# Attention sums of a graph network: indirect stores of a pair tied to TensorE's matmul groups, and TensorE's signals reduced from 16 to nine per pair

## Chip, cores and metric

One core of a Trainium2 chip runs the whole program in one launch. The metric is the device time in microseconds of one execution. Engines are called PE (TensorE), DVE (VectorE), ACT (ScalarE), POOL (GpSimd) and SP (SyncE), as in the profile; L1208 is line 1208 of the kernel.

## What is computed

Two graph layers over 100,000 nodes with 64 features and 25,000 edges sorted by target node, each followed by a residual and a layer norm. The change lies in the first layer, an attention layer with four heads and a self loop at each node:

```python
alpha = a_src_n[src2] + a_dst_n[dst2] + a_edge
alpha = jnp.where(alpha >= 0, alpha, NEG_SLOPE * alpha)
ae = jnp.exp(alpha - segment_max(alpha, dst2)[dst2])
attn = ae / segment_sum(ae, dst2)[dst2]
agg = segment_sum(xw[src2] * attn[:, :, None], dst2)
proj = (agg.reshape(n, H * C) + bias) @ Wp + bp
h = x + elu(proj)
out = layernorm(h) * gamma + beta          # then x = layernorm(x + out)
```

## The kernel before

The program has stages with a barrier between them. The **dense stage** computes the first layer for all nodes as if they had only their self loop, and gathers the rows of both ends of all edges with indirect loads that POOL issues (L277). The weights of all edges follow. Then comes the stage of the **attention sums** (names that begin with first_), which this case is about: for the nodes that have edges it forms the sums over them and writes the finished rows over the dense ones in the node table x1 in HBM (x_table in the rows). Last comes the stage of the second layer (second_), which gathers from that table.

The attention sums treat 50 units of 512 edges as 25 **pairs**. A pair stands in tiles of 128 partitions by 512 columns: 64 features of a unit from the lower half of the edges, and 64 of one from the upper half. `slots(PAIRS, 5, slot)` writes every engine's program out as 30 **slots**. In slot u each engine does its part of several pairs at different depths: `u.back(2)` is the pair two slots before. The order within a slot is the order of the calls in each engine's `slot` function, and engines meet only through semaphores.

- DVE in slot u: `own_part` (L1379) and four `product`s (L1385), one per head, write five operands `first_zb` of pair u; two `scan`s (L1392) run the weighted sums along the edges of pair u-1; `refine_roots`, `scale`, `flag`, `add_scaled` and `finish` (L1445) make the output rows of pair u-3 and u-4; `elu` and `residual` (L1411) go on with pair u-1. `finish` fills one of four row buffers `first_xr` and signals `xr_made`.
- PE in slot u: `spread` (L1231) broadcasts a head's weights over 128 partitions for a `product` of DVE, four times; `head_sum` (L1245) multiplies the five operands into one PSUM bank; `difference` (L1237) serves pair u+1; `centre` (L1251), `variance` (L1256, eight passes of two columns) and `to_rows` (L1264 and L1265) serve pair u-2.
- ACT copies, squares and takes exponentials: `square` (L1329) waits for `centre` of the same pair, `guess_roots` (L1343) for `variance`.
- POOL writes the rows of pair u-4 in slot u: eight indirect stores (here **scatters**, L1208) of 128 rows of 65 values each, addressed by `first_rows`. It waits once, for `xr_made` of the pair, and issues the eight one after the other.
- SP loads the masks and weights (`first_mask`, `first_wt`) of pair u+1 when the scans of pair u-1 are done.

PE signals by incrementing a semaphore at the end of a matmul: four times for `spread`, once for `difference`, five times for `head_sum`, once each for `centre` and `variance`, four times for `to_rows`, 16 in all for a pair.

POOL has the same kind of work in the dense stage. There a function `after_matmuls` already ties the gathers to PE's groups, here in its own words:

```python
for j in range(8):
    after_matmuls(2 * e - 3 + j // 4, j % 4)
    gather_pair(pool, e, j)
```

Of the kernel before, what the change touches and what calls it, by code (L numbers as in the profile page):

```python
# [35 lines left out]
PAIRS = UNITS // 2  # L36
# [135 lines left out]
def gnn(nc, x, gidx, drow, dblk, eaT, ea3, p64, p128, out):  # L172
# [14 lines left out]
    with ExitStack() as ctx:  # L187
# [939 lines left out]
        with ExitStack() as ph:  # L1127
# [72 lines left out]
            @block.gpsimd  # L1200
            def _(pool):
                last_row = pool.alloc_register("last_row")
                pool.reg_mov(last_row, N - 1)

                def scatter(u, s):
                    b, at = u.off % 4, (PAIRS - 1 - u.off) * 8 + 4 * s
                    for j in range(4):
                        pool.indirect_dma_start(  # L1208
                            out=x1, out_offset=bass.IndirectOffsetOnAxis(ap=first_rows[:, at + j:at + j + 1], axis=0),
                            in_=xr[b][:, 2 * j + s, :], in_offset=None, bounds_check=last_row, oob_is_err=False)\  # L1210
                            .then_inc(scattered[b], 16)

                def slot(u):
                    u = u.back(4)
                    if u.valid(PAIRS):
                        pool.wait_ge(xr_made, u.count(1))
                        scatter(u, 0)
                        scatter(u, 1)

                slots(PAIRS, 5, slot)  # L1220
                for b in range(4):
                    pool.wait_ge(scattered[b], 128 * ((PAIRS + 3 - b) // 4))

            @block.tensor
            def _(pe):
# [14 lines left out]
                def head_sum(u, n):  # L1240
                    b = u.off % 2
                    if n == 0:
                        atleast(pe, scanned, 2 * u.count(-1))
                    pe.wait_ge(z_made, u.count(0) * (H + 1) + (n + 1))
                    nc.tensor.matmul(pY[b][:, :], Mhead[:, n - 1, :] if n else Mblk[:, :], zb[n][:, :],  # L1245
                                     start=(n == 0), stop=(n == H)).then_inc(z_used, 1)

# [12 lines left out]
                def to_rows(u, j):  # L1260
# [3 lines left out]
                    nc.tensor.matmul(pG[:, c], hc[:, c], CG[:, :], start=True, stop=True)  # L1264
                    nc.tensor.matmul(pC[:, c], xd[u.off % 4][:, c], Cm, start=True, stop=True).then_inc(rows_made, 1)  # L1265

# [38 lines left out]
            def _(act):  # L1305
# [3 lines left out]
                def copy_targets(u):  # L1309
                    atleast(act, rows_made, u.count(-3) * 4)  # L1310
                    nc.scalar.activation(xd[u.off % 4][0:64, :], XT[64:128, columns(u, 0)], ACT.Identity,
# [14 lines left out]
                def square(u):  # L1326
                    act.wait_ge(hc_made, u.count(1))
                    atleast(act, rows_made, u.count(0) * 4)
                    nc.scalar.activation(sq[:, :], pH[:, :], ACT.Square, bias=ncbeta[:, :])  # L1329
# [44 lines left out]
            def _(dve):  # L1374
                def own_part(u):
                    dve.wait_ge(w_loaded[u.off % 2], u.halves(1) * 64)
                    dve.wait_ge(xd_copied, u.count(1))
                    atleast(dve, z_used, u.count(-1) * (H + 1) + 1)
                    nc.vector.scalar_tensor_tensor(zb[0][:, :], mask[u.off % 2][:, :], 1.0, xd[u.off % 4][:, :],  # L1379
                                                   ALU.subtract, ALU.mult).then_inc(z_made, 1)  # L1380

                def product(u, h):
                    dve.wait_ge(spread_made, u.count(0) * H + (h + 1))
                    atleast(dve, z_used, u.count(-1) * (H + 1) + (h + 2))
                    nc.vector.tensor_tensor(zb[1 + h][:, :], pB[h % 2][:, :], df[u.off % 2][:, :], ALU.mult).then_inc(z_made, 1)  # L1385

                def scan(u, s):
                    b, half = u.off % 2, slice(64 * s, 64 * s + 64)
                    dve.wait_ge(z_used, u.count(1) * (H + 1))
                    atleast(dve, e_made, u.count(-1))  # L1390
# [36 lines left out]
                def scale(u):  # L1427
                    dve.wait_ge(roots_made, u.count(1))
                    dve.wait_ge(rows_made, u.count(1) * 4)
                    atleast(dve, yc_made, u.count(0))  # L1430
# [709 lines left out]
```

## Time and profile before

| | us |
|---|---|
| median of 3 runs | 1848.58 |
| lowest, highest | 1843.01, 1853.82 |
| the profiled execution | 1859.29 |
| its span | 1857.5 |
| PE busy | 1280.9 (69%) |
| DVE busy | 1202.5 (65%) |
| ACT busy | 876.8 (47%) |
| POOL busy | 994.5 (54%) |
| L1208, 200 scatters, busy | 202.3 |
| granted clock of TensorE, mean share of full | 0.805 |

The attention sums lie between about 800 and 1215 us of the span. An instruction's row names the line, the operation, the tile that it writes and those that it reads. The bracket at the end is how long its engine was idle before it and what ended that. "remote" there means that the profile names no instruction of this core whose end fits the moment at which the wait ended. Starts and durations of matmuls are modelled.

### The profile page before, as it was taken

To read this page: it belongs to the slowest core of one execution; us is meant where nothing else is said; L and a number is where in the kernel's file an instruction comes from. 1 tells how busy PE (TensorE), PEld (TensorE's weight loads), DVE (VectorE), ACT (ScalarE), POOL (GpSimd) and SP (SyncE) were. 2 spreads that over 40 slices of the span, in tenths; PEclk is the share of its full clock that TensorE was granted. 3 is DMA by queue.
4 is the path that set the end of the run, shared out by engine and by line. 5 is a ranking of instruction groups with operands and counts; after the bars stand their busy time and mean duration, and the time that the engine had idled before them with its cause. 6 is when DMAs were issued, how large, how long until landed. Compare 5 with 4: busy or idle time off the path is not lost. (4 is left out here: it accounts for less than half of the span.)

```text
span 1857.5 us, 19719 instructions
## 1 busy us (share of the span) xinstructions
PE 1280.9 (69%) x5229; PEld 791.0 (43%) x5253; DVE 1202.5 (65%) x2284; ACT 876.8 (47%) x1944; POOL 994.5 (54%) x993
## 2 busy tenths in 40 slices
PE   5887787787787782068888887427667666666662
PEld 4555555555555551023444444314343344333331
DVE  4767667667667676857776777318475566665574
ACT  2667667657666673034444443405343344443341
POOL 5655555555555530003555555555676666776665
PEclk9898898888899896579888888558777777777776
DMA  4445545555545542011111111113122222222310
GB/s 114 138 149 170 156 142 169 160 152 163 165 142 162 163 135 95 0 28 30 44 51 46 44 43 44 27 38 69 36 67 50 59 61 62 61 61 50 74 46 22
DMA packets 162058, 161.98 MB, mean 87 GB/s; under 512 B 82994, under 2 KB 99681, under 8 KB 161948
## 3 DMA queue, kind: packets, MB, share of 16 engines
q1 hardware_dynamic: 130300, 130.80, 22.8%
q0 software_dynamic: 31648, 29.92, 7.7%
q8 instruction: 43, 0.70, 0.2%
q14 instruction: 67, 0.55, 0.1%
HBM read 66.88 MB, written 83.27 MB: 81 GB/s over the span
## 5 line engine op out<-in xcount | busy, mean ns | idle before, releaser
L277 POOL DMA_INDIRECT ids_pairs<-in_x_dram,gix x392 | 383.7, 979 | 296.9 <-PE bank L605 149.5
L1208 POOL DMA_INDIRECT x_table<-first_xr,first_rows x200 | 202.3, 1011 | 331.8 <-DVE first_xr L1445 273.3
L1605 POOL DMA_INDIRECT second_raw<-x_table,gix x196 | 201.0, 1026 | 142.7 <-PE twin L1711 60.8
L1611 POOL DMA_INDIRECT out_dram<-second_orow,last_rows x196 | 202.5, 1033 | 70.8 <-issue 58.5
L587 PE MATMUL twin<-AC,dense_hb 128*128 128x256 f32 x784 | 198.1, 397 | 37.7 <-DVE dense_hb L741 25.5
L579 PE MATMUL bank<-dense_xT,Mblk 128*128 128x512 f32 x196 | 125.6, 727 | 71.5 <-ACT dense_rl L670 53.2
L587 PEld LDWEIGHTS twin<-AC,dense_hb 128*128 128x128 f32 x784 | 147.0, 198 | 64.9 <-DVE dense_hb L741 31.4
L749 DVE TENSOR_REDUCE dense_v<-dense_q 128x8 f32<-128x512 f32 x98 | 66.7, 681 | 110.7 <-ACT dense_q L645 108.9
L1245 PE MATMUL twin<-first_zb,Mhead 128*128 128x512 f32 x200 | 129.3, 736 | 0.0
L595 PE MATMUL bank<-prm,dense_xT 128*128 128x128 f32 x784 | 118.5, 300 | 2.4 <-DVE dense_yc L784 2.3
L1385 DVE TENSOR_TENSOR first_zb<-twin,first_df 128x512 f32<-128x512 f32 x100 | 66.6, 686 | 79.0 <-remote 58.8
L595 PEld LDWEIGHTS bank<-prm,dense_xT 128*128 128x128 f32 x784 | 110.9, 218 | 4.7 <-DVE dense_yc L784 3.5
L681 ACT ACTIVATE dense_hq<-twin 128x512 f32<-128x512 f32 x98 | 58.7, 599 | 98.2 <-PE twin L587 63.6
L1787 ACT ACTIVATE second_decay<-twin 128x512 f32<-128x512 f32 x25 | 14.9, 597 | 184.7 <-issue 158.6
L729 DVE TENSOR_REDUCE dense_v<-dense_hq 128x8 f32<-128x512 f32 x98 | 66.8, 682 | 29.9 <-issue 15.7
L695 ACT ACTIVATE dense_lrow<-bank 12x512 f32<-12x512 f32 x50 | 29.3, 587 | 120.1 <-remote 115.1
L570 PEld LDWEIGHTS bank<-prm,ids_rows 128*128 128x128 f32 x392 | 58.1, 162 | 64.2 <-issue 64.2
L784 DVE TENSOR_TENSOR dense_yc<-dense_yb,bank 128x512 f32<-128x512 f32 x98 | 66.6, 679 | 26.2 <-issue 26.2
L741 DVE SCALAR_TENSOR_TENSOR dense_hb<-dense_xT,nbeta,dense_gb 128x512 f32<-128x512 f32 x98 | 73.7, 752 | 11.8 <-issue 0.5
L675 ACT ACTIVATE dense_xT<-bank,prm 128x512 f32<-128x512 f32 x98 | 67.3, 687 | 28.7 <-remote 28.7
L579 PEld LDWEIGHTS bank<-dense_xT,Mblk 128*128 128x128 f32 x196 | 35.3, 215 | 99.9 <-issue 78.1
L1108 DVE TENSOR_REDUCE d_s<-XT 128x8 f32<-128x512 f32 x50 | 31.9, 678 | 70.3 <-ACT XT L1077 57.5
(360 smaller groups left out, 3072.5 us busy)
## 6 DMA issues: line engine op xcount, KB each, us to landing
x_table<-dense_yc SPq DMA_DIRECT2D x98, 260.0 KB
ids_rows<-in_x_dram SPq DMA_DIRECT2D x98, 256.0 KB
out_dram<-dense_orow SPq DMA_DIRECT2D x98, 256.0 KB
XT<-dense_turned SPq DMA_DIRECT2D x50, 256.0 KB
target_rows<-first_xr SPq DMA_DIRECT2D x50, 128.0 KB
ids_pairs<-in_x_dram,gix POOLq DMA_INDIRECT x392
second_targets<-target_rows SPq DMA_DIRECT2D x49, 128.0 KB
first_mask<-mask_rows SPq DMA_DIRECT2D x50, 64.0 KB
```

The source lines that it names most:

```text
L277: pool.indirect_dma_start(out=pairs[e % 2][:, j % 4, F * (j // 4):F * (j // 4) + F], out_offset=None, in_=x, in_offset=bass.IndirectOffset ...
L579: nc.tensor.matmul(pP[:, :], Mblk[:, :], xT[u.off % 4][:, :], start=True, stop=True).then_inc(p_made, 1)
L587: last = nc.tensor.matmul(pGC[b][:, j * 256:(j + 1) * 256], hb[b][:, j * 128:(j + 1) * 128], AC[:, :], start=True, stop=True)
L595: last = nc.tensor.matmul(pX[:, c], xT[u.off % 4][:, c], Cm, start=True, stop=True)
L675: nc.scalar.activation(xT[u.off % 4][:, :], pT[:, :], ACT.Identity, bias=c128("beta")).then_inc(x_copied, 1)
L729: nc.vector.tensor_reduce(v[b][:, 0:8], hq[b][:, :, :], AX.X, ALU.add).then_inc(v1_made, 1)
L741: nc.vector.scalar_tensor_tensor(hb[b][:, :], xT[u.off % 4][:, :], nbeta[:, :], gb[:, :], ALU.add, ALU.add)\
L749: nc.vector.tensor_reduce(v[b][:, 8:16], q2[b][:, :, :], AX.X, ALU.add).then_inc(s2_made, 1)
L1208: pool.indirect_dma_start(out=x1, out_offset=bass.IndirectOffsetOnAxis(ap=first_rows[:, at + j:at + j + 1], axis=0), in_=xr[b][:, 2 * j + ...
L1245: nc.tensor.matmul(pY[b][:, :], Mhead[:, n - 1, :] if n else Mblk[:, :], zb[n][:, :], start=(n == 0), stop=(n == H)).then_inc(z_used, 1)
L1605: pool.indirect_dma_start(out=raw[u.off % 3][:, 2 * j + s, :], out_offset=None, in_=x1, in_offset=bass.IndirectOffsetOnAxis(ap=gix[:, at:a ...
L1611: pool.indirect_dma_start(out=out, out_offset=bass.IndirectOffsetOnAxis(ap=last_rows[:, at:at + 1], axis=0), in_=orow[u.off % 4][:, 2 * j ...
```

## The change

POOL's scatter function calls a new `after_matmuls` before each of the eight scatters. The scatters of pair k are issued while the engines work on pairs k+4 and k+5, and six of the calls wait, counted for pair k+5: scatter 2 (counting from 0) for `z_used`, that is for all head sums up to pair k+4; scatters 3, 4, 6 and 7 for the first, second, third and fourth `spread` of pair k+5; scatter 5 is tied to `hc_made`, the `centre` of pair k+3. Scatters 0 and 1 have no wait of their own. For the last five pairs there is no pair k+5 and nothing is tied.

`head_sum` signals only with its last matmul, and `to_rows` only with its last: nine signals for a pair in place of 16. All counts that wait on them are rewritten. Where DVE waited, before overwriting an operand `first_zb`, for the head sum of the pair before that read this operand, it now waits in `own_part` for all head sums of that pair, and the products no longer wait for `z_used`.

```diff
--- before.py
+++ after.py
@@ -1202,9 +1202,19 @@
                 last_row = pool.alloc_register("last_row")
                 pool.reg_mov(last_row, N - 1)
 
+                def after_matmuls(u, part):
+                    if u.valid(PAIRS):
+                        if part == 2:
+                            pool.wait_ge(z_used, u.count(0))
+                        if part in (3, 4, 6, 7):
+                            pool.wait_ge(spread_made, H * u.count(0) + {3: 1, 4: 2, 6: 3, 7: 4}[part])
+                        if part == 5:
+                            pool.wait_ge(hc_made, u.count(-1))
+
                 def scatter(u, s):
                     b, at = u.off % 4, (PAIRS - 1 - u.off) * 8 + 4 * s
                     for j in range(4):
+                        after_matmuls(u.back(-5), 4 * s + j)
                         pool.indirect_dma_start(
                             out=x1, out_offset=bass.IndirectOffsetOnAxis(ap=first_rows[:, at + j:at + j + 1], axis=0),
                             in_=xr[b][:, 2 * j + s, :], in_offset=None, bounds_check=last_row, oob_is_err=False)\
@@ -1242,8 +1252,10 @@
                     if n == 0:
                         atleast(pe, scanned, 2 * u.count(-1))
                     pe.wait_ge(z_made, u.count(0) * (H + 1) + (n + 1))
-                    nc.tensor.matmul(pY[b][:, :], Mhead[:, n - 1, :] if n else Mblk[:, :], zb[n][:, :],
-                                     start=(n == 0), stop=(n == H)).then_inc(z_used, 1)
+                    last = nc.tensor.matmul(pY[b][:, :], Mhead[:, n - 1, :] if n else Mblk[:, :], zb[n][:, :],
+                                            start=(n == 0), stop=(n == H))
+                    if n == H:
+                        last.then_inc(z_used, 1)
 
                 def centre(u):
                     pe.wait_ge(h_made, u.count(1))
@@ -1262,7 +1274,9 @@
                         atleast(pe, yc_made, u.count(0))
                     c = slice(j * 128, (j + 1) * 128)
                     nc.tensor.matmul(pG[:, c], hc[:, c], CG[:, :], start=True, stop=True)
-                    nc.tensor.matmul(pC[:, c], xd[u.off % 4][:, c], Cm, start=True, stop=True).then_inc(rows_made, 1)
+                    last = nc.tensor.matmul(pC[:, c], xd[u.off % 4][:, c], Cm, start=True, stop=True)
+                    if j == 3:
+                        last.then_inc(rows_made, 1)
 
                 def slot(u):
                     if u.static() and u.count(0) == 0:
@@ -1307,7 +1321,7 @@
                     name=nc.get_next_instruction_name(), engine=mybir.EngineType.Activation, act_func_set_id=EXP_AND_LN))
 
                 def copy_targets(u):
-                    atleast(act, rows_made, u.count(-3) * 4)
+                    atleast(act, rows_made, u.count(-3))
                     nc.scalar.activation(xd[u.off % 4][0:64, :], XT[64:128, columns(u, 0)], ACT.Identity,
                                          bias=c128("beta")[64:128, :])
                     nc.scalar.activation(xd[u.off % 4][64:128, :], XT[64:128, columns(u, 1)], ACT.Identity,
@@ -1325,7 +1339,7 @@
 
                 def square(u):
                     act.wait_ge(hc_made, u.count(1))
-                    atleast(act, rows_made, u.count(0) * 4)
+                    atleast(act, rows_made, u.count(0))
                     nc.scalar.activation(sq[:, :], pH[:, :], ACT.Square, bias=ncbeta[:, :])
                     nc.scalar.activation(hc[:, :], pH[:, :], ACT.Identity, bias=ncbeta[:, :]).then_inc(sq_made, 1)
 
@@ -1375,18 +1389,17 @@
                 def own_part(u):
                     dve.wait_ge(w_loaded[u.off % 2], u.halves(1) * 64)
                     dve.wait_ge(xd_copied, u.count(1))
-                    atleast(dve, z_used, u.count(-1) * (H + 1) + 1)
+                    atleast(dve, z_used, u.count(0))
                     nc.vector.scalar_tensor_tensor(zb[0][:, :], mask[u.off % 2][:, :], 1.0, xd[u.off % 4][:, :],
                                                    ALU.subtract, ALU.mult).then_inc(z_made, 1)
 
                 def product(u, h):
                     dve.wait_ge(spread_made, u.count(0) * H + (h + 1))
-                    atleast(dve, z_used, u.count(-1) * (H + 1) + (h + 2))
                     nc.vector.tensor_tensor(zb[1 + h][:, :], pB[h % 2][:, :], df[u.off % 2][:, :], ALU.mult).then_inc(z_made, 1)
 
                 def scan(u, s):
                     b, half = u.off % 2, slice(64 * s, 64 * s + 64)
-                    dve.wait_ge(z_used, u.count(1) * (H + 1))
+                    dve.wait_ge(z_used, u.count(1))
                     atleast(dve, e_made, u.count(-1))
                     atleast(dve, crossed, u.count(0) * 2 + (1 - s))
                     nc.vector.tensor_tensor_scan(ys[b][half, ::-1], mask[b][half, ::-1], pY[b][half, ::-1],
@@ -1426,7 +1439,7 @@
 
                 def scale(u):
                     dve.wait_ge(roots_made, u.count(1))
-                    dve.wait_ge(rows_made, u.count(1) * 4)
+                    dve.wait_ge(rows_made, u.count(1))
                     atleast(dve, yc_made, u.count(0))
                     nc.vector.tensor_tensor(yb[:, :, :], pG[:, :].rearrange("p (r f) -> p r f", f=F),
                                             w[:, 0:8].unsqueeze(2).to_broadcast([128, 8, F]), ALU.mult).then_inc(scaled, 1)
```

POOL's program around the stage, before: the last pair of the attention sums and what comes behind (first_xr_made is the signal of `finish`).

```order
L1208 DMA x_table<-first_xr,first_rows 100000x65 [waits first_xr_made]
L1208 DMA x_table<-first_xr,first_rows 100000x65 x7
L1127 UNCONDITIONAL_BRANCH [waits first_scattered2,first_scattered3,first_scattered1,first_scattered0]
L1598 UNCONDITIONAL_BRANCH [waits barrier_Pool_Activation_PE_DVE_SP_gather]
L1638 DMA second_lead<-x_table,gix 128x65 [waits second_cleared]
```

POOL after the change, from the stage's first row on: the first pair.

```order
L1200 UNCONDITIONAL_BRANCH [waits barrier_Pool_Activation_PE_DVE_SP_gather]
L1218 DMA x_table<-first_xr,first_rows 100000x65 [waits first_xr_made]
L1218 DMA x_table<-first_xr,first_rows 100000x65
L1218 DMA x_table<-first_xr,first_rows 100000x65 [waits first_z_used]
L1218 DMA x_table<-first_xr,first_rows 100000x65 [waits first_spread_made] x2
L1218 DMA x_table<-first_xr,first_rows 100000x65 [waits first_hc_made]
L1218 DMA x_table<-first_xr,first_rows 100000x65 [waits first_spread_made] x2
```

The eight scatters keep their order and number; six of the seven that followed freely are now tied to one signal of PE each.

DVE, before, from a place in the middle of the stage: the beginning of a slot (twin is the PSUM tile that `spread` or `head_sum` wrote).

```order
L1411 TENSOR_TENSOR first_hb<-first_gb,first_xd 128x512 [waits first_xd_copied,first_g_made,first_hc_made]
L1379 SCALAR_TENSOR_TENSOR first_zb<-first_mask,first_xd 128x512 [waits first_z_used,first_xd_copied,first_w_loaded1]
L1385 TENSOR_TENSOR first_zb<-twin,first_df 128x512 [waits first_z_used,first_spread_made] x2
L1392 SCALAR_TENSOR_TENSOR first_ys<-first_mask,first_start,twin 64x512 [waits first_crossed,first_e_made,first_z_used]
L1399 COPY first_start<-first_ys 64x1 [waits first_scanned]
L1420 TENSOR_TENSOR first_off<-first_ve,first_halved 128x16 [waits first_root_steps]
```

DVE at the same place after the change.

```order
L1424 TENSOR_TENSOR first_hb<-first_gb,first_xd 128x512 [waits first_xd_copied,first_g_made,first_hc_made]
L1393 SCALAR_TENSOR_TENSOR first_zb<-first_mask,first_xd 128x512 [waits first_z_used,first_xd_copied,first_w_loaded1]
L1398 TENSOR_TENSOR first_zb<-twin,first_df 128x512 [waits first_spread_made] x2
L1405 SCALAR_TENSOR_TENSOR first_ys<-first_mask,first_start,twin 64x512 [waits first_crossed,first_e_made,first_z_used]
L1412 COPY first_start<-first_ys 64x1 [waits first_scanned]
L1433 TENSOR_TENSOR first_off<-first_ve,first_halved 128x16 [waits first_root_steps]
```

No instruction of DVE moved; the products lost their wait for first_z_used.

## Rows read from the trace of the kernel before

**Rows 1.** Busy time by stretch (us, busy and count by engine, PEclk, DMA share, GB/s).
```profile
853.00:1149.00 296.00, 247.62 (x878) 124.54 (x877) 204.62 (x360) 124.51 (x257) 162.69 (x160) 0.84 0.17 44
1017.00:1028.00 11.00, 10.72 (x47) 5.42 (x46) 10.17 (x19) 6.33 (x14) 8.07 (x8) 1.00 0.22 57
1028.00:1048.00 20.00, 12.44 (x42) 5.83 (x41) 9.88 (x18) 5.96 (x13) 8.07 (x8) 0.75 0.13 35
1048.00:1061.00 13.00, 13.00 (x47) 7.02 (x48) 10.18 (x19) 6.27 (x14) 8.21 (x8) 0.85 0.22 52
1150.00:1215.00 65.00, 28.46 (x124) 22.48 (x124) 24.01 (x52) 27.41 (x58) 39.44 (x40) 0.58 0.13 31
```

**Rows 2.** Who waited for whom, 850 to 1150 us: total us, times, longest.
```profile
ACT first_sq L1329 <- remote: 61.8, 7, 9.8
DVE first_zb L1385 <- remote: 58.8, 7, 9.3
```

**Rows 3.** GpSimd in order of time, 1016 to 1050 us (start, us, instruction, idle).
```profile
1017.72 0.97 POOL L1208 DMA_INDIRECT x_table<-first_xr,first_rows  x1 [3.17 <-DVE first_xr L1445]
...
1026.95 0.97 POOL L1208 DMA_INDIRECT x_table<-first_xr,first_rows  x1 [0.30 <-issue]
1028.75 0.97 POOL L1208 DMA_INDIRECT x_table<-first_xr,first_rows  x1 [0.83 <-DVE first_xr L1445]
1030.03 1.27 POOL L1208 DMA_INDIRECT x_table<-first_xr,first_rows  x1 [0.30 <-issue]
1031.60 0.97 POOL L1208 DMA_INDIRECT x_table<-first_xr,first_rows  x1 [0.30 <-issue]
...
1037.99 0.97 POOL L1208 DMA_INDIRECT x_table<-first_xr,first_rows  x1 [0.30 <-issue]
1049.16 0.97 POOL L1208 DMA_INDIRECT x_table<-first_xr,first_rows  x1 [10.20 <-DVE first_xr L1445]
```

**Rows 4.** VectorE in order of time, 1016 to 1043 us.
```profile
1016.76 0.68 DVE L1445 TENSOR_TENSOR first_xr<-first_yc,first_wf 128x512 f32<-128x512 f32 x1
...
1019.93 0.69 DVE L1379 SCALAR_TENSOR_TENSOR first_zb<-first_mask,first_xd 128x512 f32<-128x512 bf16 x1 [0.51 <-DMA first_mask<-mask_rows]
1020.54 1.28 DVE L1385 TENSOR_TENSOR first_zb<-twin,first_df 128x512 f32<-128x512 f32 x2
...
1027.80 0.68 DVE L1445 TENSOR_TENSOR first_xr<-first_yc,first_wf 128x512 f32<-128x512 f32 x1
...
1030.99 0.69 DVE L1379 SCALAR_TENSOR_TENSOR first_zb<-first_mask,first_xd 128x512 f32<-128x512 bf16 x1 [0.53 <-DMA first_mask<-mask_rows]
1040.95 1.29 DVE L1385 TENSOR_TENSOR first_zb<-twin,first_df 128x512 f32<-128x512 f32 x2 [9.27 <-remote]
```

**Rows 5.** TensorE matmuls in order of time, 1016 to 1043 us.
```profile
1019.95 0.60 PE L1231 MATMUL twin<-first_wt,headsel 24*128 24x512 bf16 x2 [0.28 <-DMA first_mask<-mask_rows]
...
1026.06 0.95 PE L1256 MATMUL bank<-prm,first_sq 128*128 128x2 f32 x8
...
1028.70 1.02 PE L1245 MATMUL twin<-first_zb,Mhead 128*128 128x512 f32 x2
...
1031.01 0.60 PE L1231 MATMUL twin<-first_wt,headsel 24*128 24x512 bf16 x2 [0.40 <-DMA first_mask<-mask_rows]
```

**Rows 6.** ScalarE in order of time, 1016 to 1043 us.
```profile
1030.00 0.27 ACT L1343 ACTIVATE first_ve<-bank,eps 128x8 f32<-128x8 f32 x1 [1.65 <-remote]
...
1041.03 0.69 ACT L1329 ACTIVATE first_sq<-bank,ncbeta 128x512 f32<-128x512 f32 x1 [9.83 <-remote]
```

**Rows 7.** Dense stage, order of time, 350 to 362 us: TensorE.
```profile
354.59 1.03 PE L614 MATMUL bank<-dense_eab,WalE 16*12 16x512 f32 x4
```

**Rows 8.** Dense stage, same stretch: GpSimd.
```profile
358.18 0.94 POOL L277 DMA_INDIRECT ids_pairs<-in_x_dram,gix  x1 [0.30 <-issue]
```

**Rows 9.** Dense stage, same stretch: ScalarE.
```profile
360.21 1.19 ACT L695 ACTIVATE dense_lrow<-bank 12x512 f32<-12x512 f32 x2 [5.83 <-remote]
```

**Rows 10.** ScalarE in the last slots, 1160 to 1190 us.
```profile
1181.48 0.27 ACT L1343 ACTIVATE first_ve<-bank,eps 128x8 f32<-128x8 f32 x1 [10.58 <-remote]
```

## The prediction

> **What bounds the kernel now.** I read first how long a slot of the attention sums takes, then what the engines wait for in it, and last the order of time around one wait.
>
> In steady state the stage gives one pair per slot. From 853 to 1149 us POOL issues 160 scatters, that is 20 pairs, in 296 us [rows 1]: 14.8 us per slot. But slots differ. One from 1017 to 1028 takes 11.0 us, with PE busy 10.72 us at full granted clock and DVE busy 10.17: both full. The next takes 20 us and holds no more work (DVE 9.88 us busy), the one after 13 us, at a granted clock of 0.85 [rows 1]. So 11.0 us is what the work needs, and 296 - 20 x 11.1 = 74 us is lost in 20 slots (11.1 rather than 11.0, as a slot's loads and waits vary a little).
>
> The waits say where: seven waits of DVE's first product of a slot for "remote", 58.8 us in all, and seven of ACT's square, 61.8 us, which run beside them [rows 2]. Seven of some 9 us, and behind each a slot at reduced clock, which costs the rest: 58.8 + 7 x 2 = 73 us.
>
> The order of time shows what "remote" is. At 1031.0 PE does the two spreads that the products wait for; they end at 1031.6 [rows 5]. DVE's own part began at 1030.99, so the products could begin at 1031.6; they begin at 1040.95 [rows 4]. ACT's square, which waits for a later matmul, begins within 0.1 us of them [rows 6]. The variance matmuls ended at 1027.0 [rows 5] and ACT's reader of them began at 1030.00 [rows 6], while it was idle. So the work was done and its **signals were held**, several together, to be let go together. Meanwhile POOL issued scatters: 1028.75 to 1038.96, each 0.97 to 1.27 us long and 0.3 us apart; the held products begin 2.0 us after the last of them has ended [rows 3, 4]. In the slot before, POOL's eight scatters began at 1017.72 and the spreads of 1019.95 reached DVE without loss: its products begin at 1020.54, right behind its own part [rows 3 to 5]. So scatters alone do not hold a signal. What differs: in the second case a scatter (1026.95 to 1027.92) ran while the variance matmuls ended, and POOL paused only 0.83 us before the next eight [rows 3, 5]. Then PE added signals, 16 in a slot, faster than they came through (that of the variance at 1030.0, those of the spreads at 1040.9), so the row grew until POOL stopped. I take the held row of signals as the bound of this stage, and the overlap of POOL's trains with PE's signals as its cause.
>
> **The change part by part.**
>
> Nine signals for 16: no matmul, load or operand moves. PE is not shown waiting on its own signals in the 11 us slot, so by the rows the direct worth is nothing. The Trainium skill ("TensorE: Matmul & The Clock Gate", The cost: per-tile semaphore tail) says that increments serialize at about 26 ns each; 7 x 25 pairs would give an estimate of 4.6 us, and the sum would be that much lower. No row here shows it. What the smaller number does by the rows is to keep the held row short: between the variance and the first spread of the next slot there stood the head sums' last two and four of to_rows; now one of each.
>
> The six waits of POOL: 120 in all, for 20 pairs. In an undisturbed slot they cost nothing. Scatter 0 leaves 0.24 us after `finish` has ended, at +0; scatter 2 followed at about +2.85 (1031.60 against 1028.75) [rows 3]; the last head sum ends 1.0 us after scatter 0 begins (1028.70 + 1.02 against 1028.75) and the next spreads at +2.9 [rows 3, 5], so the signals for scatters 2, 3 and 4 are there or all but there when POOL comes to them, and those for the later ones likewise, since POOL needs 1.28 us per scatter. The cover is POOL's own pace; were it gone, each wait would delay one scatter, and behind it only `finish` waits, for a buffer four pairs old.
>
> In a slot whose signals are held, the waits are what counts. Scatters 0 and 1 still go at once (1028.75 to 1031.30). Scatter 2 now needs the last head sum's signal, which stands in the held row, so POOL stops at 1031.30 where it went on to 1038.96. How long after a stop is the row let go? The near rows give 2.0 us here, and 1.1 us in the dense stage: the last gather ended at 359.12, and ACT's L695, which had waited 5.83 us for matmuls that ended at 355.6, began at 360.21 [rows 7 to 9]. So the signals arrive at 1032.4 to 1033.3. New here is that DVE's own part waits for the same head sum; it can only begin then, and the products 0.6 us later, 1033.0 to 1033.9 against an undisturbed 1031.6: 1.4 to 2.3 us. If the head sum's signal slips through alone and starts scatter 2 with the spreads still held, one scatter (1.27) is added: up to 3.6 us. Below, the bound is 0, that the row is never held. I take 1.9 us, near the middle of the first pair, since its upper end is measured in this stage. DVE has 0.5 us of slack in a slot (its wait for `first_mask`, 0.53 [rows 4]), which I leave out, as the loads shift too. Such a wait is a fifth of the present one, and PE idles for 2 us instead of 7, so I also drop the slot at reduced clock.
>
> How many slots are so disturbed? Now it is seven of 20, each followed by a long gap of POOL (10.20 us [rows 3]) that clears the way for two. After the change the gap is short, so the pattern returns sooner: between every slot and every other. I take two in three. Mean slot: 11.1 + 2/3 x 1.9 = 12.4 us; 20 slots 247 us; **gain 296 - 247 = 49 us**.
>
> The end, 1150 to 1215 us [rows 1]: the last five pairs are not tied, and the 10.58 us wait of ACT there stays [rows 10]. With one signal of to_rows for four, the row is shorter behind it: gain 0 to 3 us, I take 1. The dense and the second-layer stages are untouched: 0.
>
> Sum: 49 + 1 = 50 us. The profiled execution took 1859.3 us (span 1857.5), 10.7 above the median, and would take 1809; from the median, 1848.6 - 50 = **1799 us**.
>
> **The rivals.** A difference of 0.5%, 9 us, is about what a measurement of this kernel can tell from none.
>
> B. *Signals are no longer held at all.* The overlap of train and variance signal may need the long unbroken row of scatters, and the shorter row of signals may never build up. For it: six of POOL's eight scatters now come behind a signal that has come through. Against: scatters 6 and 7 still fall where they fell, beside the variance matmuls. Every slot 11.1: gain 74, 1775 us or, with the end, 1774.
>
> C. *Held more often and longer.* Every slot is disturbed, and the row is let go as late as 2.8 us: 13.9 us per slot, 278 us, gain 18, 1831 us. For it: the dense stage, where POOL's gathers are tied in the same manner, still shows a wait of 5.83 us [rows 9]. Against: there the gathers before 359.12 went on in spite of the held row; here scatter 2 waits for a member of it.
>
> D. *Nothing that can be told.* If what holds the signals is not POOL's train but, say, the traffic of the stores already issued, the same seven waits stay: 1848.6, give or take 9.
>
> E. *Slower: tied scatters hold the next signal.* Each tied scatter begins at the moment a PE signal arrives, the next signal comes during it, and is held until POOL has stopped: a chain of six, each 1.27 us of scatter and 1.1 to 2.0 us of release. With 2.55 us for the first two, a slot would be 2.55 + 6 x 2.8 = 19.4 us, loss 20 x 4.6 = 92 us, 1940 us. It decides from the point where a step takes more than (14.8 - 2.55)/6 = 2.0 us. For it: a train takes 10.2 of 11 us, so POOL has 0.83 us to spare [rows 3], and any wait that is late by more pushes the next train. The Trainium skill ("DMA: Bandwidth & Descriptors", Rules for kernel authors) has a rule on this side: issue a transfer early and wait for it late. Against it: the slot from 1017 us, in which the spreads ended within a train and nothing was held [rows 3 to 5].
>
> **How the numbers follow.** A, my forecast, 0.50; its own range, mean slots of 11.7 to 13.2 us, is 1786 to 1816. B 0.22, C 0.14, D 0.08, E 0.06. The predicted time is A's. The range takes in A, B (its end is 1774, so 1773) and C with some more: to 1838; outside lie D, E and little else, less than 0.2. Faster by over 0.5%: A, B and most of C, 0.85. Within 0.5%: D and the rest of C, 0.09. Slower: 0.06.
>
> **What the profile of the changed kernel would show.** The seven "remote" waits of 9 us before L1398 (now the products) gone, and in their place waits of 1 to 3 us before the own part or the products; the same on ACT's square. POOL's trains with a pause behind scatter 1 or 2 in those slots, and without one in the others. The pairs' scatters at 12.4 us per eight from 853 us on, the stage ending near 1165 rather than 1215 us. The granted clock near full up to the last slots. PE's and DVE's busy time per slot unchanged, apart from the clock. The 10.6 us wait at the end still there. The forecast is wrong if waits of 5 us or more remain between 853 and 1100 us, if slots of 13 us at full clock are the rule, or if pauses of POOL stand in slots in which no signal was late.

## The result, and the profile after

| | before | after |
|---|---|---|
| median | 1845.8 us (4 runs) | 1799.1 us (4 runs) |
| lowest, highest | 1837.0, 1853.8 | 1790.6, 1807.4 |
| profiled execution | 1859.29 us | 1800.23 us |
| its span | 1857.5 us | 1798.4 us |

The ratio is 0.974, with a 95% interval of 0.970 to 0.978: 47 us less in the medians, 59 in the two profiled executions.

The page of the kernel after, its span, the busy time of PE and the granted clock in 40 slices:

```profile
span 1798.4 us, 19623 instructions
...
PE 1254.3 (70%) x5229; PEld 773.6 (43%) x5253; DVE 1202.0 (67%) x2284; ACT 877.7 (49%) x1944; POOL 997.8 (55%) x993
...
PEclk9888998989989889559999997568777777777876
```

The attention sums of the kernel after, in three stretches: the first slots, the 20 slots in which POOL issues the scatters of 20 pairs, and the end (columns as in [rows 1]):

```profile
805.00:857.00 52.00, 48.75 (x149) 18.95 (x150) 34.91 (x57) 20.13 (x38) 0.00 (x0) 0.87 0.05 12
857.00:1097.00 240.00, 219.28 (x887) 108.87 (x886) 205.60 (x362) 126.06 (x259) 165.89 (x160) 0.99 0.22 55
1097.00:1163.00 66.00, 29.10 (x124) 23.70 (x124) 23.98 (x52) 27.37 (x58) 38.90 (x40) 0.59 0.13 31
```

The first slots of the kernel before, which were not shown:

```profile
805.00:853.00 48.00, 45.32 (x150) 18.46 (x151) 35.40 (x58) 20.62 (x39) 0.00 (x0) 0.95 0.05 13
```

So 20 pairs take 240 us where they took 296 [rows 1], 12.0 us per slot where it was 14.8, with PE's granted clock at 0.99 where it was 0.84, and the same busy time on DVE (205.60 against 204.62 us). The first slots grew from 48 to 52 us and the end from 65 to 66. From 805 us on the stage is 52 us shorter. The remaining 7 us between the two profiled executions lie in stages that the change does not touch, and are less than runs of one kernel differ by.

Who waited for "remote" in the 20 slots of the kernel after (total us, times, longest):

```profile
ACT first_ve L1357 <- remote: 13.7, 5, 4.1
...
DVE first_zb L1393 <- remote: 13.3, 7, 2.2
...
POOL x_table L1218 <- remote: 10.7, 9, 1.5
```

Against [rows 2] the seven waits of 8.4 us on average before a product are gone. Seven waits of DVE's own part stand in their place, 1.9 us each, and nine of POOL, 1.2 us each. One of them in order of time: POOL, DVE and PE of the kernel after, around 978 us (L1218 is the scatter, L1393 the own part, L1398 a product, L1255 a head sum, L1241 a spread, L1268 the variance).

```profile
975.21 0.97 POOL L1218 DMA_INDIRECT x_table<-first_xr,first_rows  x1 [0.30 <-issue]
977.08 0.97 POOL L1218 DMA_INDIRECT x_table<-first_xr,first_rows  x1 [0.90 <-issue]
978.35 1.27 POOL L1218 DMA_INDIRECT x_table<-first_xr,first_rows  x1 [0.30 <-issue]
981.10 1.39 POOL L1218 DMA_INDIRECT x_table<-first_xr,first_rows  x1 [1.47 <-remote]
982.80 0.97 POOL L1218 DMA_INDIRECT x_table<-first_xr,first_rows  x1 [0.30 <-issue]
```

```profile
980.95 0.69 DVE L1393 SCALAR_TENSOR_TENSOR first_zb<-first_mask,first_xd 128x512 f32<-128x512 bf16 x1 [2.17 <-remote]
981.56 1.28 DVE L1398 TENSOR_TENSOR first_zb<-twin,first_df 128x512 f32<-128x512 f32 x2
```

```profile
974.39 0.95 PE L1268 MATMUL bank<-prm,first_sq 128*128 128x2 f32 x8
...
977.03 1.02 PE L1255 MATMUL twin<-first_zb,Mhead 128*128 128x512 f32 x2
...
979.30 0.60 PE L1241 MATMUL twin<-first_wt,headsel 24*128 24x512 bf16 x2 [0.35 <-DMA first_mask<-mask_rows]
```

The variance matmuls end at 975.34, inside a scatter. The last head sum ends at 978.05, the spreads at 979.90. POOL issues scatters 0 and 1, until 979.62, and stops, since the signal of the head sums has not come. DVE's own part begins at 980.95, POOL's scatter 2 at 981.10, the products at 981.56. This is the picture of [rows 3 to 5] with POOL's train cut short after two scatters.

### The profile page after: what moved, and what is told of

It is laid out like the page before. It is cut to its first block and busy times, and to the rows that moved or that the text cites. A ratio compares the mean times of both kernels' runs of the same rounds, so it can differ in the third digit from the quotient of the medians.

```text
span 1798.4 us, 19623 instructions
## 1 busy us (share of the span) xinstructions
PE 1254.3 (70%) x5229; PEld 773.6 (43%) x5253; DVE 1202.0 (67%) x2284; ACT 877.7 (49%) x1944; POOL 997.8 (55%) x993
## 5 line engine op out<-in xcount | busy, mean ns | idle before, releaser
L1218 POOL DMA_INDIRECT x_table<-first_xr,first_rows x200 | 205.4, 1027 | 277.0 <-DVE first_xr L1458 200.8
L1255 PE MATMUL twin<-first_zb,Mhead 128*128 128x512 f32 x200 | 110.8, 639 | 0.6 <-DVE first_zb L1398 0.4
L1728 PE MATMUL bank<-prm,second_num 128*128 128x128 f32 x100 | 23.3, 376 | 93.0 <-issue 81.0
L741 DVE SCALAR_TENSOR_TENSOR dense_hb<-dense_xT,nbeta,dense_gb 128x512 f32<-128x512 f32 x98 | 73.7, 752 | 11.8 <-issue 0.5
```

Of the source, the lines that this page charges most:

```text
L741: nc.vector.scalar_tensor_tensor(hb[b][:, :], xT[u.off % 4][:, :], nbeta[:, :], gb[:, :], ALU.add, ALU.add)\
L1218: pool.indirect_dma_start(out=x1, out_offset=bass.IndirectOffsetOnAxis(ap=first_rows[:, at + j:at + j + 1], axis=0), in_=xr[b][:, 2 * j + ...
L1255: last = nc.tensor.matmul(pY[b][:, :], Mhead[:, n - 1, :] if n else Mblk[:, :], zb[n][:, :], start=(n == 0), stop=(n == H))
```

## The experiments

Twelve runs were made, of six kernels, in six jobs. The jobs turned out to be of two sorts, which decides what each run can tell, so that comes first.

### Nine signals alone, POOL's waits alone, no scatters, another tie: first job

The first kernel is the change without the function `after_matmuls`:

```diff
-                        after_matmuls(u.back(-5), 4 * s + j)
```

> The nine signals per pair of the change, with POOL's scatters free as before. Theory (a held row of signals is let go only when POOL stops, and before that one signal comes through in about 1.4 us): the first spread is the fourth in the row rather than the eighth, so the waits of the products shrink from 9 to about 3 to 6 us but stay; 1815 to 1835 us. Rival 1 (the number of signals alone is the cause): 1799 us, as the whole change. Rival 2 (signals play no part): 1846 us.

The second is the kernel before with `after_matmuls`, its count for the head sums adapted to 16 signals:

```diff
+                            pool.wait_ge(z_used, u.count(0) * (H + 1))
...
+                        after_matmuls(u.back(-5), 4 * s + j)
```

> The six waits of POOL, with the 16 signals of before. Theory: POOL stops behind scatter 1 whenever the row is held, whatever the row's length, so the waits are 2 us as in the whole change; 1795 to 1810 us. Rival 1 (the number of signals is the cause): near 1846 us. Both fall if it is over 1860 us.

The third leaves out POOL's part of the stage and DVE's wait for it:

```diff
-                        pool.indirect_dma_start(
-                            out=x1, out_offset=bass.IndirectOffsetOnAxis(ap=first_rows[:, at + j:at + j + 1], axis=0),
-                            in_=xr[b][:, 2 * j + s, :], in_offset=None, bounds_check=last_row, oob_is_err=False)\
...
-                    atleast(dve, scattered[b], u.quarters(0) * 128)
```

> The changed kernel without the scatters of the attention sums (it leaves out the store of the finished rows into the node table; the second layer reads the dense ones). Theory (POOL's scatters hold the signals): no wait for remote is left in this stage, every slot 11.1 us, which is 17 us less over 20 slots, some 15 us less in the last slots, and some 12 us less since the last rows need no store: 1750 to 1765 us. Rival 3 (signals are late whatever POOL does): slots of 12.0 us stay, 1785 us or more.

The fourth moves scatter 7 behind the variance:

```diff
-                        if part in (3, 4, 6, 7):
-                            pool.wait_ge(spread_made, H * u.count(0) + {3: 1, 4: 2, 6: 3, 7: 4}[part])
+                        if part in (3, 4, 6):
+                            pool.wait_ge(spread_made, H * u.count(0) + {3: 1, 4: 2, 6: 3}[part])
+                        if part == 7:
+                            pool.wait_ge(var_made, u.count(-1))
```

> The changed kernel with scatter 7 tied to the signal of the variance matmuls in place of the fourth spread. Theory with a trigger (a row begins to be held when the variance's signal meets a scatter): scatter 7 moves behind it, by 0.3 us, no signal is held before scatter 0 of the next pair, slots 11.2 to 11.5 us, 1782 to 1792 us. Rival 4 (any signal can begin a held row): no better, 1795 to 1805 us.

Measured: the kernel before took 1560.8 us in this job, 285 us less than in the runs above. Against it the nine signals gave 1.001 (0.999 to 1.003), POOL's waits 1.000 (0.998 to 1.002), the other tie 1.002 (1.000 to 1.004), and the kernel without scatters 0.989 (0.987 to 0.992), 1544 us. None of the expectations on held signals could be tried: there were none. The kernel with nine signals and free scatters, in the same places as [rows 3 to 5]:

```profile
862.91 0.97 POOL L1208 DMA_INDIRECT x_table<-first_xr,first_rows  x1 [0.30 <-issue]
864.72 0.97 POOL L1208 DMA_INDIRECT x_table<-first_xr,first_rows  x1 [0.83 <-DVE first_xr L1448]
866.11 1.15 POOL L1208 DMA_INDIRECT x_table<-first_xr,first_rows  x1 [0.42 <-issue]
867.57 0.97 POOL L1208 DMA_INDIRECT x_table<-first_xr,first_rows  x1 [0.30 <-issue]
```

```profile
862.03 0.95 PE L1258 MATMUL bank<-prm,first_sq 128*128 128x2 f32 x8
...
867.00 0.60 PE L1231 MATMUL twin<-first_wt,headsel 24*128 24x512 bf16 x2 [0.42 <-DMA first_mask<-mask_rows]
```

```profile
866.98 0.69 DVE L1383 SCALAR_TENSOR_TENSOR first_zb<-first_mask,first_xd 128x512 f32<-128x512 bf16 x1 [0.56 <-DMA first_mask<-mask_rows]
867.59 1.28 DVE L1388 TENSOR_TENSOR first_zb<-twin,first_df 128x512 f32<-128x512 f32 x2
```

A scatter begins at 862.91, the variance ends at 862.98, POOL pauses 0.83 us and goes on at 864.72: to 0.1 us the situation of 1026.95 us in the kernel before. There DVE lost 9.3 us. Here the own part begins at 866.98 and the products right behind it, at 867.59. So the meeting of a scatter and a signal, in which I had seen the cause, does not by itself hold a signal.

### The whole change once more

> The whole change once more, beside the kernel before on the same chip. In the run of the first four experiments no signal of TensorE was held at all, and the kernel before took 1561 us. Theory: the worth of the change is the held signals. If the kernel before takes about 1846 us here, its ratio is 0.974 again; if it takes about 1561 us and no signal is held, the ratio is 1.00, between 0.997 and 1.004, the slots 11.1 to 11.3 us. Rival (the change has a worth of its own, by fewer signals and waits): 0.99 or less on either.

Measured: 1755.0 us against 1795.2 us of the kernel before, ratio 0.976 (0.968 to 0.983). This was a job of the other sort, and the worth of the change was there again; in its profile the 20 slots took 236 us, 11.8 each. The rival (0.99 or less on either) is not excluded by this job: what speaks against it is that the two halves of the change gave 1.001 and 1.000 in the first one. The whole change was never timed in a job without held signals.

### The first three kinds in a job with held signals

> The nine signals alone once more, for a chip on which signals are held (the kernel before near 1790 to 1850 us). Theory: the row is let go only when POOL stops, so waits of 3 to 6 us stay before the products; ratio 0.982 to 0.994. Rival 1 (the number of signals alone is the cause): 0.975, as the whole change. Rival 2 (it plays no part): 1.00. Where no signal is held: 1.00.

> The six waits of POOL with the 16 signals of before, once more. Theory: POOL stops behind scatter 1 while a row is held, however long it is; ratio 0.973 to 0.980, waits of 1 to 3 us before the products, slots of 12 us. Rival 1 (the number of signals): 0.99 to 1.00. Where no signal is held: 1.00.

> Scatter 7 tied to the variance's signal in place of the fourth spread's, once more. Theory with a trigger (the row begins where the variance's signal meets scatter 7): slots of 11.2 to 11.5 us in place of 11.9, 8 to 14 us less than the whole change, ratio 0.967 to 0.971. Rival 4 (any signal that meets a scatter can begin a row): 0.973 to 0.978.

The kernel before took 1848.1 us here.

**Nine signals alone**: 1842.9 us, 0.993 (0.986 to 0.999). The view of who waited in its 20 slots (847 to 1136 us), and the busy time by stretch; L1383 is the own part and L1388 a product in this kernel.

```profile
ACT first_sq L1333 <- remote: 74.0, 8, 10.2
...
DVE first_zb L1383 <- remote: 39.1, 9, 7.1
...
DVE first_zb L1388 <- remote: 22.4, 9, 3.5
```

```profile
100.00:500.00 400.00, 315.68 (x1528) 219.65 (x1527) 288.21 (x587) 266.26 (x649) 233.34 (x237) 0.92 0.51 161
847.00:1136.00 289.00, 245.72 (x883) 116.10 (x883) 204.98 (x361) 125.14 (x258) 163.89 (x160) 0.89 0.17 46
```

The 20 slots take 289 us, 14.5 us each. DVE has 18 waits, 61.5 us in all, where it had seven, 58.8 us in all [rows 2]: nine pairs wait twice, first before the own part and then before the products. One of them, with the last scatter of the train:

```profile
896.26 1.09 POOL L1208 DMA_INDIRECT x_table<-first_xr,first_rows  x1 [0.30 <-issue]
```

```profile
895.81 0.69 DVE L1383 SCALAR_TENSOR_TENSOR first_zb<-first_mask,first_xd 128x512 f32<-128x512 bf16 x1 [7.08 <-remote]
899.31 1.29 DVE L1388 TENSOR_TENSOR first_zb<-twin,first_df 128x512 f32<-128x512 f32 x2 [2.81 <-remote]
```

The scatter ends at 897.35, the products begin 1.96 us later. In the first of the two waits the head sums' signal, in the second the spreads' was missing. The first ended while POOL's train still went on, and so did all nine before the own part and three of the nine before the products; the other six ended 0.1 to 2.0 us behind the last scatter. So "let go only when POOL stops" is too strong: some signals come through before.

Nor is the row shorter in time. By the trace's records of the semaphores 6.5 us pass from the variance's signal (889.24) to that of the last head sum (895.69). In the kernel before, at the place of [rows 5, 6], it was 6.6 us (1029.98 to 1036.55), although PE there signalled three more times between the two. At two further places of the kernel before and four of this one it was 5.8 us. The theory's ratio, 0.982 to 0.994, holds at its weak end, but not its reason, waits that shrink; the rival that the number of signals is the cause (0.975) falls. That the number plays no part (1.00) lies just outside the interval.

**POOL's waits alone**, with 16 signals: 1797.9 us, 0.979 (0.970 to 0.989).

```profile
849.00:1086.00 237.00, 216.33 (x882) 108.66 (x881) 205.44 (x361) 125.18 (x258) 160.37 (x160) 0.99 0.22 55
```

```profile
968.74 0.97 POOL L1218 DMA_INDIRECT x_table<-first_xr,first_rows  x1 [0.77 <-DVE first_xr L1455]
970.02 1.27 POOL L1218 DMA_INDIRECT x_table<-first_xr,first_rows  x1 [0.30 <-issue]
972.50 0.97 POOL L1218 DMA_INDIRECT x_table<-first_xr,first_rows  x1 [1.22 <-remote]
```

```profile
971.01 0.69 DVE L1389 SCALAR_TENSOR_TENSOR first_zb<-first_mask,first_xd 128x512 f32<-128x512 bf16 x1 [0.57 <-DMA first_mask<-mask_rows]
972.41 1.29 DVE L1395 TENSOR_TENSOR first_zb<-twin,first_df 128x512 f32<-128x512 f32 x2 [0.71 <-PE twin L1241]
```

20 slots in 237 us, 11.9 each, where the whole change had 12.0. POOL stops at 971.29 and the products begin 1.12 us later; the own part (L1389) is not late, since here it waits for an older head sum. The waits do what the whole change does. The nine signals add nothing to them that can be told: the kernel with both and one tie moved, next in this job, took 1796.9 us.

**Scatter 7 behind the variance**: 1796.9 us, 0.974 (0.964 to 0.984), slots of 11.9 us. The interval takes in both expectations. Against the theory with a trigger, 0.967 to 0.971, speaks the profile: slots of 11.2 to 11.5 us were expected.

```profile
997.45 0.95 PE L1270 MATMUL bank<-prm,first_sq 128*128 128x2 f32 x8
```

```profile
998.46 0.97 POOL L1220 DMA_INDIRECT x_table<-first_xr,first_rows  x1 [0.30 <-issue]
999.74 0.97 POOL L1220 DMA_INDIRECT x_table<-first_xr,first_rows  x1 [0.30 <-issue]
1002.74 0.97 POOL L1220 DMA_INDIRECT x_table<-first_xr,first_rows  x1 [2.04 <-remote]
```

```profile
1002.50 0.27 ACT L1359 ACTIVATE first_ve<-bank,eps 128x8 f32<-128x8 f32 x1 [3.07 <-remote]
```

The variance ends at 998.40, between two scatters. Scatters 5 and 6 follow at once, and its reader on ACT (L1359) begins at 1002.50, 1.8 us after POOL has stopped. The pause of POOL only moved from behind scatter 1 to ahead of scatter 7.

### The wait for the head sums moved to scatter 0

```diff
-                        if part == 2:
+                        if part == 0:
                             pool.wait_ge(z_used, u.count(0))
```

> The changed kernel with the wait for the head sums moved from scatter 2 to scatter 0; the other five waits stay. Theory (a row is let go 1 to 2 us after POOL stops): POOL now stops right behind scatter 7 when a row is held, so the row is gone by the time the spreads of the next pair come; DVE's own part is not late; slots of 11.1 to 11.5 us where signals are held, 8 to 16 us less than the whole change, ratio 0.966 to 0.971. Rival: POOL's train starts 1 us later in every slot and runs into the next one, slots of 12 us or more, ratio 0.975 or above. Where no signal is held: 1.00.

> The wait for the head sums at scatter 0 rather than scatter 2, once more, for a chip on which signals are held. Theory: POOL stops right behind scatter 7 when a row is held, slots of 11.1 to 11.5 us, ratio 0.966 to 0.971, no wait of DVE for remote over 1 us before the own part or the products. Rival: the train starts 1 us later in every slot and runs into the next, slots of 12 us or more, ratio 0.975 or above.

The first run fell in a job without held signals (kernel before 1562.0 us): 1.001 (0.999 to 1.002). The second: 1767.9 us against 1797.1, ratio 0.987 (0.980 to 0.995), worse than the whole change had in its two jobs. In the second, 20 slots take 247 us, 12.3 each:

```profile
951.38 1.02 PE L1255 MATMUL twin<-first_zb,Mhead 128*128 128x512 f32 x2
```

```profile
951.50 1.10 POOL L1218 DMA_INDIRECT x_table<-first_xr,first_rows  x1 [0.30 <-issue]
952.91 0.97 POOL L1218 DMA_INDIRECT x_table<-first_xr,first_rows  x1 [0.30 <-issue]
956.12 0.97 POOL L1218 DMA_INDIRECT x_table<-first_xr,first_rows  x1 [2.25 <-remote]
```

```profile
955.50 0.69 DVE L1393 SCALAR_TENSOR_TENSOR first_zb<-first_mask,first_xd 128x512 f32<-128x512 bf16 x1 [1.76 <-remote]
```

The last head sum (L1255) ends at 952.40, under scatter 6; scatter 7 follows. POOL stops at 953.88, and its signal reaches DVE's own part at 955.50, 1.6 us later. The train starts later in the slot, so another signal meets its end. The rival's numbers were right (12 us or more, 0.975 or above), and no version was found that beats the change.

### No scatters, twice more

> The changed kernel without the scatters of the attention sums (it leaves out the store of the finished rows into the node table), once more, for a chip on which signals are held. Theory: no wait for remote in this stage, every slot 11.1 us, and the long waits of the last slots gone too; ratio 0.945 to 0.96. In the stages in which POOL still issues indirect transfers the waits for remote stay. Rival 3 (signals are late whatever POOL does): slots of 12 us, ratio 0.965 or above.

> The changed kernel without the scatters of the attention sums (it leaves out the store of the finished rows into the node table), a third time, since no signal was held in the first two. If the kernel before takes about 1790 to 1850 us here: by the theory no wait for remote in this stage, slots of 11.1 to 11.2 us, ratio 0.945 to 0.96, while the stages with indirect transfers keep theirs; by the rival (signals are late whatever POOL does) slots of 12 us and 0.965 or above. If the kernel before takes about 1561 us: 0.989 as before, which tells nothing of it.

Both fell in jobs in which the kernel before took 1562 us: 1547.1 and 1545.4 us, 0.989 each time (0.986 to 0.992). They tell what the scatters cost where no signal is held: 15 to 16 us, and nothing of it in the 20 slots.

```profile
707.00:930.00 223.00, 213.48 (x886) 107.97 (x885) 204.07 (x361) 125.62 (x258) 0.00 (x0) 1.00 0.15 38
```

223 us for 20 slots, against 224 of the kernel with scatters in such a job (below). The kernel without scatters was never seen with held signals; that experiment is open. The nearest to it lies in the traces that are there. Between the dense stage's last gather and the first scatter, from 681 to 854 us in the kernel before, POOL issues nothing; the same stretch is 173 to 177 us long in the seven traces from jobs with held signals. PE signals 66 to 94 times in it, and no engine waits for remote in any of the seven, but for one wait of ACT that ended 1.4 us behind the last gather.

## Why the prediction was right

The forecast was 1799 us, measured 1799.1. Point by point:

- **The bound.** That held signals cost 74 us in 20 slots and 11.1 us is what the work needs: shown. In jobs without held signals the same slots take 11.2 us (224 us for 20, at granted clock 1.00), with scatters as free as before. The cause that I gave, the overlap of POOL's trains with PE's signals, is not enough: the same overlap stands in those jobs and nothing is held.
- **Nine for 16: nothing by itself.** Nearly: 0.993 alone in a job with held signals (5 us by the medians, 14 by the ratio), nothing in one without. The estimate of 4.6 us that I worked out from the Trainium skill ("TensorE: Matmul & The Clock Gate", The cost: per-tile semaphore tail) does not show: where nothing is held, the interval of 0.999 to 1.003 allows a gain of 1 us at most, and where signals are held it can't be told from the rest. That fewer signals keep the held row short was wrong: 6.5 against 6.6 us for the same stretch of it. With POOL's waits there, nothing of their worth is left.
- **POOL's waits cut the wait to 1.4 to 2.3 us, taken as 1.9.** DVE's seven waits are 13.3 us: 1.9 each, of which some 0.5 would be the wait for the mask in any slot. The release came sooner than the 1.1 to 2.0 us taken from [rows 3, 4] and [rows 7 to 9]: the seven own parts begin 0.7 to 1.4 us after POOL's stop. In the experiments 1.12, 1.6, 1.8 and 1.96 us were read.
- **Mean slot 12.4 us.** It was 12.0, and the 20 slots took 240 us where the sum had 247. What was mis-sized is the product of share and wait: two in three times 1.9 is 25 us, and DVE's waits are seven in 20 slots, 13.3 us, of which the mask's 0.5 us, left out in the sum, can be 3.5. The 20 slots are 18 us above 20 x 11.1, so 5 to 8 us were lost in another way, which the sum did not have. A part is PE: the slot at reduced clock, which I dropped, is not quite gone, since the granted clock is at its lower level for some us behind two of the waits (0.57 from 910 to 914 and from 982 to 986 us). The rest was not traced.
- **The first slots: 0.** They cost 4 us in this pair of profiles. The own part now waits for all head sums of the pair before, and in the first slots nothing covers that wait: in the second pair of the kernel after it stands as 2.80 us, where before it began right behind the product. That this wait makes the 4 us isn't shown: from the stage's first own part to its first scatter the eight executions with the new wait take 49.1 to 53.2 us, the three with the old one 48.8 to 50.8. Rows of DVE, kernel after:

```profile
811.08 0.69 DVE L1398 TENSOR_TENSOR first_zb<-twin,first_df 128x512 f32<-128x512 f32 x1 [3.58 <-PE twin L1241]
813.62 0.69 DVE L1398 TENSOR_TENSOR first_zb<-twin,first_df 128x512 f32<-128x512 f32 x1 [1.85 <-PE twin L1241]
817.11 0.69 DVE L1393 SCALAR_TENSOR_TENSOR first_zb<-first_mask,first_xd 128x512 f32<-128x512 bf16 x1 [2.80 <-PE twin L1255]
```

- **The end: gain 1.** It was a loss of 1 us, 65 to 66 us. The waits of the untied pairs are there as forecast, two long ones of ACT among them:

```profile
1106.85 0.69 ACT L1343 ACTIVATE first_sq<-bank,ncbeta 128x512 f32<-128x512 f32 x1 [7.49 <-remote]
...
1133.80 1.08 ACT L1077 ACTIVATE XT<-twin 128x512 f32<-128x512 f32 x2 [6.85 <-remote]
```

- In the profiled pair these errors do not cancel: 50 + 7 - 4 - 2, and 7 us of stages not touched, is 58, and the pair shows 59. The medians show 47. That the forecast met the median to 0.1 us is luck, the more as a fourth run moved the median of the kernel before from 1848.6 to 1845.8 us.
- A small misreading without effect: scatter 0 leaves 0.27 us after `finish` has ended (1027.80 + 0.68), not 0.24.
- **The rivals.** B (no signal is held at all) did not come about through the change. It is the case in three of the seven jobs, where each half of the change alone is worth nothing (1.001 and 1.000). C fell: slots of 12.0 us, not 13.9, and the longest wait of DVE for a held signal in the 20 slots is 2.2 us (of ACT 4.1). E fell: slots between 11.0 and 13.6 us, none of 19. D fell as it was put, since tying POOL alone brings the gain. But part of it stands: something besides POOL's train decides whether signals are held.

What is shown and what is not. Shown: tying POOL brings the gain (0.979 alone) and reducing the signals hardly any (0.993 alone). Seen in the traces: where POOL stops, held signals come through soon after, in the one place read in each of six kernels 1.1 to 2.0 us later (before 2.0, after 1.3, and 1.1, 1.6, 1.8 and 2.0 in the experiments); and where POOL has issued nothing for 2 us or more before the first scatter, none is late. But some come through before POOL stops, one of the seven products of [rows 2] among them (at 963.24 us). Not shown: that without scatters no signal is held in such a job, and whether it is POOL's issuing or the traffic of its stores that holds them, since a stop of POOL ends both. Not known: what makes one job hold them.

## What to carry to other kernels

When several engines start together some microseconds after the work that they waited for was done, read the semaphore wait against the end of the matmul, and look at which engine stopped just before: here a pause of POOL of one or two microseconds, placed by a wait for the very signals that are late, turned seven waits of 8.4 us into seven of 1.9. Such a wait is nearly free if the engine would have come to the transfer only when the signal is there anyway: where no signal was held, the six waits gave 1.000. Time the kernel before again in each job: POOL's waits were worth 2% in one and nothing in another, and a profile of one job shows only one of them.

## What was not expected of the hardware

The same kernel, with nine signals and free scatters, was profiled in both sorts of job. In the job of 1561 us (the rows of the job of 1848 us stand under "Nine signals alone"):

```profile
100.00:500.00 400.00, 366.68 (x1932) 256.49 (x1930) 361.20 (x744) 334.96 (x816) 289.37 (x298) 1.00 0.66 203
707.00:931.00 224.00, 213.32 (x885) 107.74 (x884) 203.93 (x361) 125.37 (x258) 162.38 (x160) 1.00 0.23 59
```

The dense stage, which has waits of POOL in both, does 1932 matmuls in the 400 us from 100 on, against 1528 in the same stretch of the other job, at a granted clock of 1.00 against 0.92; and its 20 slots of the attention sums take 224 against 289 us. In the slower one, waits for remote stand in all three stages that have indirect transfers; in the faster one the trace has none. It is not the chip alone: two chips were met in both sorts, one with the kernel before at 1795.2 and then 1562.0 us, another at 1797.1 and then 1561.6 us. What it is, no run here shows. Of the 285 us by which the kernel before is slower in the job of the first table (1845.8 against 1560.8) the change gives back 47.

The release has a pace of its own. By the trace's records of the semaphores in the kernel before, most of the held signals that came through while POOL went on did so in steps of 1.4 to 1.5 us or twice that (1032.89, 1034.36, 1035.82, 1039.44), although scatters begin every 1.28 us. Those that were left came together once POOL had stopped, 30 to 60 ns apart: the readers on DVE and ACT start at 1040.95 and 1041.03 [rows 4, 6]. It is not a pace per signal, since with three signals fewer the same stretch took as long.
